# A two-layer graph convolution kernel: row blocks of each h added by an accumulating transfer before the column sums

## The reference, cut to what matters

```python
h = jnp.maximum(_layernorm(x, axis=-1), 0.0)
x = x + _L0_gnn_ref(h, adj, L0_gnn_b1, adj, L0_gnn_b2)

# inside _L0_gnn_ref
fv = x.mean(axis=1)                      # column means of h
nf = fv / norm(fv); sim = nf[:, :, None] * nf[:, None, :]
_, idx = top_k(sim, 9); idx = idx[..., 1:]
adj = zeros.at[b, row, idx].set(1.0); adj = max(adj, adj.T); diag = 1
h = relu(_gc(swapaxes(x), adj, W1, b1))  # (adj / deg) @ (x @ W.T + b)
h = _gc(h, adj, W2, b2)
```

## Time and profile before

| what | value |
|---|---|
| median of 3 runs | 506.15 us (505.9 to 506.9) |
| profiled execution, own time | 505.98 us |
| its span | 503.8 us |
| busy: TensorE, POOL, VectorE, ScalarE | 484.9, 372.7, 357.3, 339.2 us |
| mean granted TensorE clock | 0.992 of full speed |
| moved by DMA | 102.74 MB, 204 GB/s in the mean |

### The profile page before, as it was taken

One profiled execution on the slowest core, in us unless ns is written; L12 is line 12 of the kernel. 1 busy time (PEld: TensorE's weight loads), 2 busy tenths in 40 slices (PEclk: granted clock), 3 DMA queues, 4 the chain that ended last, 5 costly groups with the idle time before them and its releaser, 6 DMA issues.

```text
span 503.8 us, 7367 instructions
## 1 busy us (share of the span) xinstructions
PE 484.9 (96%) x2434; PEld 332.4 (66%) x2434; DVE 357.3 (71%) x891; ACT 339.2 (67%) x699; POOL 372.7 (74%) x343
## 2 busy tenths in 40 slices
PE   1998999999999999999999999999999999999996
PEld 0256577667776777757776777767776677777774
DVE  5999897988776886788776887778766764522334
ACT  4747888658777587757788487758877565545551
POOL 0356549959779697769878697777879697797772
PEclk9997999999999999999999999999999999999999
DMA  8992376356566465646666266646444243444424
GB/s 328 349 378 85 146 272 240 111 220 245 209 251 251 155 241 212 242 164 262 250 246 249 91 260 252 236 183 251 175 169 147 94 160 127 154 167 168 167 85 167
DMA packets 27717, 102.74 MB, mean 204 GB/s; under 512 B 2080, under 2 KB 2592, under 8 KB 27680
## 3 DMA queue, kind: packets, MB, share of 16 engines
q1 hardware_dynamic: 27296, 101.23, 53.0%
q0 software_dynamic: 384, 1.05, 0.6%
HBM read 68.72 MB, written 33.55 MB: 203 GB/s over the span
## 4 chain that ended last, share of the span: by engine, by line
PE 88%; DVE 8%; DMA 2%; ACT 1%; issue 1%; SPq 0%; DVEq 0%; ACTq 0%
PE ps L599 48%; PE ps L605 24%; PE ps L629 5%; PE aux L564 5%; PE aux L660 4%; DVE stats L733 2%; DMA xin<-x 2%; PE aux L588 1%; DVE onehot L818 1%; DVE code_r L798 1%; DVE res L911 1%; PE aux L575 1%; DVE onehot L807 1%; PE ps L636 0%; DVE code L764 0%
## 5 line engine op out<-in xcount | busy, mean ns | idle before, releaser
L474 POOL TENSOR_TENSOR r_lo<-r,r_hi 128x512 fp32r<-128x512 f32 x128 | 162.7, 1294 | 46.8 <-ACT r_hi L383 45.3
L463 POOL TENSOR_TENSOR h_lo<-hb,h_hi 128x512 fp32r<-128x512 f32 x128 | 167.9, 1325 | 7.0 <-ACT h_hi L346 7.0
L911 DVE SCALAR_TENSOR_TENSOR res<-ps,bias,res 128x512 f32<-128x512 f32 x128 | 90.2, 747 | 77.4 <-PE ps L636 77.3
L599 PE MATMUL ps<-r_hi,w_hi 128*128 128x512 f32 x256 | 108.7, 425 | 1.3 <-ACT r_hi L375 1.3
L599 PE MATMUL ps<-h_hi,w_hi 128*128 128x512 f32 x256 | 102.0, 399 | 0.3 <-DVE res L911 0.3
L599 PE MATMUL ps<-r_hi,w_lo 128*128 128x512 f32 x256 | 102.1, 399 | 0.0
L599 PE MATMUL ps<-h_hi,w_lo 128*128 128x512 f32 x256 | 101.3, 396 | 0.0
L324 ACT ACTIVATE hb<-xin,nmean,rstd 128x1024 f32<-128x1024 f32 x64 | 79.0, 1235 | 32.4 <-DVE nmean L754 32.4
L366 ACT ACTIVATE r<-ps,beta 128x512 f32<-128x512 f32 x64 | 43.4, 684 | 74.4 <-PE ps L629 74.4
L733 DVE BATCH_NORM_STATS2 stats<-xin 128x6 f32<-128x512 f32 x128 | 79.1, 678 | 3.8 <-DMA xin<-x 3.8
L605 PE MATMUL ps<-h_lo,w_hi 128*128 128x512 f32 x256 | 73.3, 408 | 0.0
(11 more groups left out here) (94 smaller groups left out, 545.7 us busy)
## 6 DMA issues: line engine op xcount, KB each, us to landing
res<-x SPq DMA_DIRECT2D x32, 1024.0 KB, 4.8
out<-res SPq DMA_DIRECT2D x31, 1024.0 KB, 4.0
xin<-x SPq DMA_DIRECT2D x30, 1024.0 KB, 7.1
xin<-x SPq DMA_DIRECT2D x4, 512.0 KB, 5.1
out<-res SPq DMA_DIRECT2D x4, 256.0 KB, 2.1
w<-w_t SPq DMA_DIRECT2D x1, 256.0 KB, 9.1
cst<-small SPq DMA_DIRECT2D x1, 229.0 KB, 6.9
xg<-x_t,rows POOLq DMA_INDIRECT x8, 4.8
```

What stands on the lines that cost most here:

```text
L463: last = nc.gpsimd.tensor_tensor(h_lo[:, kf, n], hb[:, b % NH, kf, n], h_hi[:, kf, n].bitcast(F32), ALU.subtract)
L474: last = nc.gpsimd.tensor_tensor(r_lo[:, kf, n], r[:, kf, n], r_hi[:, kf, n].bitcast(F32), ALU.subtract)
L599: nc.tensor.matmul(bank[m][:], wt[:, kf, m * P:m * P + P], mov[:, kf, n], start=(kf == 0 and wt is w_hi), stop=False, skip_group_check=True)
L911: nc.vector.scalar_tensor_tensor(res[:, b % NR, m, n], bank[m][:], bias2[:, m:m + 1], res[:, b % NR, m, n], ALU.add, ALU.add).then_inc(out ...
```

## The change

- `column_sums(k)` for k = 2 to 7 streams one block per batch, `h_sum[:, q]`, in place of two. For k = 1 it stays as it was.
- `h_sum` holds four blocks. For each batch from 8 to 31 SP copies the first row block of h into it (`copy_h`, SBUF to SBUF, 512 KB), and POOL issues a transfer that adds the second block to it (`fold`, 512 KB, `accum_op=add`). TensorE waits for the four folds of the group. Before batch 8, h_sum is the load buffer of x of batches 3 and 7.
- The ring of x has three buffers, without those two batches. load_x(11) waits for batch 8 to be normalised, where it waited for batch 7.
- On TensorE `column_sums(k)`, k > 1, stands behind layer2(t, 1).
- ScalarE normalises batch t+9 in step t, behind split_h(t+2, 0) and take_sums, where it normalised batch t+8 at the head of the step. It raises `h_first` after the first block. VectorE's moments and scales run a batch further ahead.
- ScalarE writes `code` and `ZERO` straight from the sums in PSUM (`zeros`: Relu of 0.5 - 2^112 s is 0.5 for a sum of zero and 0 else) and the class codes are renumbered to fit; VectorE's pass for `code` goes. It keeps a small `stat`, now with a row sum, and adds 6 to it in `top_rows`.
- TensorE's waits for take_sums become waits for `zeros`.

The diff without its blank lines and most of its context:

```diff
@@ -19,7 +19,7 @@
 G = 4
-NX = 4
+NX = 3
@@ -47,6 +47,12 @@
+CODES = [1.0, 1.5, 2.0, 3.0, 0.0, 0.5, 6.0, 7.0]
+HALF = 0.5
+STEEP = -(2.0 ** 112)
@@ -59,7 +65,7 @@
     parts = [
-        ("cls", np.where(row < 16, row % 8, -1.0)[:, None]),
+        ("cls", np.where(row < 16, np.array(CODES)[row % 8], -1.0)[:, None]),
@@ -102,6 +108,7 @@
         hb = sb("hb", [P, NH, KF, N])
+        h_sum = sb("h_sum", [P, G, N])
@@ -123,10 +130,12 @@
         eps = sb("eps", [P, 1])
+        half = sb("half", [P, 1])
...
         best = sb("best", [P, 8])
+        stat = sb("stat", [P, K_TOP])
@@ -160,7 +169,7 @@
         STAT = aux[:, at + 72:at + 72 + K_TOP]
-        ZERO = aux[:, at + 80:at + 81]
+        ZERO = aux[:, N - 1:N]
@@ -176,6 +185,17 @@
+        def turn(b):
+            return b - (b > G - 1) - (b > 2 * G - 1)
+        def x_of(b):
+            if b in (G - 1, 2 * G - 1):
+                i = 2 * (b // G)
+                return h_sum[:, i:i + 2]
+            return xin[:, turn(b) % NX]
@@ -196,6 +216,10 @@
         h_ready = sem("h_ready")
+        h_first = sem("h_first")
+        side_loaded = [sem(f"side_loaded{i}") for i in range(2)]
+        copied = [sem(f"copied{q}") for q in range(G)]
+        folded = sem("folded")
@@ -268,9 +292,18 @@
             def load_x(b):
-                if b >= NX:
-                    sp.wait_ge(h_ready, b - NX + 1)
-                sp.dma_start(xin[:, b % NX], x_v[b]).then_inc(x_loaded[b % NX], 16)
+                if b in (G - 1, 2 * G - 1):
+                    sp.dma_start(x_of(b), x_v[b]).then_inc(side_loaded[b // G], 16)
+                else:
+                    if b >= NX:
+                        sp.wait_ge(h_ready, b - NX + (b >= LEAD + NX))
+                    sp.dma_start(x_of(b), x_v[b]).then_inc(x_loaded[turn(b) % NX], 16)
+            def copy_h(b):
+                sp.wait_ge(h_first, b - LEAD + 1)
+                sp.wait_ge(fv_done, 2 * (b // G))
+                sp.dma_start(h_sum[:, b % G], hb[:, b % NH, 0]).then_inc(copied[b % G], 16)
@@ -283,19 +316,26 @@
             sp.dma_start(w[:], w_t.rearrange("(k p) n -> p k n", p=P)).then_inc(w_loaded, 16)
-            load_x(3)
+            load_x(G - 1)
...
             sp.dma_start(bias2[:], b2).then_inc(bias_loaded, 16)
-            for b in range(NX, LEAD):
+            for b in range(G, LEAD):
...
                 load_res(b)
-            for b in range(LEAD, LEAD + NX - 1):
+            for b in range(LEAD, LEAD + NX):
...
             for t in range(NB):
-                if t + LEAD + NX - 1 < NB:
-                    load_x(t + LEAD + NX - 1)
+                if t + LEAD + NX < NB:
+                    load_x(t + LEAD + NX)
+                if t == 1:
+                    copy_h(LEAD)
+                    copy_h(LEAD + 1)
+                if t == 2:
+                    copy_h(LEAD + 2)
+                if 1 < t < NB - LEAD - 1:
+                    copy_h(t + LEAD + 1)
@@ -322,12 +362,14 @@
                 last = nc.scalar.activation(
-                    hb[:, a, kf], xin[:, b % NX, kf], ACT.Relu, bias=nmean[:, kf, e:e + 1],
+                    hb[:, a, kf], x_of(b)[:, kf], ACT.Relu, bias=nmean[:, kf, e:e + 1],
...
                     last.then_inc(h_part, 1)
+                elif b >= LEAD:
+                    last.then_inc(h_first, 1)
@@ -337,6 +379,14 @@
+            def zeros(k):
+                com = dict(bias=half[:], scale=STEEP)
+                act.wait_ge(fv_copied, 3 * k + 3)
+                nc.scalar.activation(code[:, K_TOP + 1:H + 1], aux[:, K_TOP:H], ACT.Relu, **com)
+                nc.scalar.activation(code[:, H + 1:N], aux[:, H:N - 1], ACT.Relu, **com)
+                nc.scalar.activation(ZERO, aux[:, N - 1:N], ACT.Relu, **com).then_inc(zero_ready, 1)
@@ -396,6 +446,7 @@
             split_h(1, 0)
+            zeros(0)
@@ -408,24 +459,30 @@
             for t in range(LAST):
-                if 0 < t < NB - LEAD:
-                    normalise(t + LEAD, 0)
-                    normalise(t + LEAD, 1)
+                if t == 1:
+                    normalise(LEAD + 1, 0)
+                    normalise(LEAD + 1, 1)
...
                     root(7)
+                if t + 2 < NB:
+                    split_h(t + 2, 0)
...
                     take_sums(group_at(t, 0))
-                if t + 2 < NB:
-                    split_h(t + 2, 0)
+                    zeros(group_at(t, 0))
...
                     root(LEAD + 2)
+                elif 1 < t < NB - LEAD - 1:
+                    normalise(t + LEAD + 1, 0)
+                    normalise(t + LEAD + 1, 1)
+                    if t == 2:
+                        root(LEAD + 4)
@@ -434,12 +491,16 @@
                 if t == 0:
+                    zeros(1)
...
                     normalise(LEAD, 1)
+                    root(LEAD + 1)
...
                     root(LEAD + 3)
-                elif t != 2 and t + LEAD + 1 < NB:
-                    root(t + LEAD + 1)
+                    normalise(LEAD + 2, 0)
+                    normalise(LEAD + 2, 1)
+                elif 2 < t < NB - LEAD - 2:
+                    root(t + LEAD + 2)
@@ -482,6 +543,11 @@
+            def fold(b):
+                pool.wait_ge(copied[b % G], 16 * (b // G - 1))
+                pool.wait_ge(h_ready, b + 1)
+                nc.gpsimd.dma_start(h_sum[:, b % G], hb[:, b % NH, 1], accum_op=ALU.add).then_inc(folded, 16)
@@ -532,9 +598,16 @@
                         split_h(3, 0)
+                if t == 1:
+                    fold(LEAD)
+                    fold(LEAD + 1)
+                elif 1 < t < NB - LEAD - 1:
+                    fold(t + LEAD + (t > 2))
...
                     split_h(t + 2, 1)
+                if t == 2:
+                    fold(LEAD + 3)
@@ -555,21 +628,26 @@
             def column_sums(k):
-                pe.wait_ge(h_ready, G * k + G)
+                if k == 1:
+                    pe.wait_ge(h_ready, 2 * G)
+                else:
+                    pe.wait_ge(folded, 16 * G * (k - 1))
                 pe.wait_ge(beta_ready, k)
+                blocks = KF if k == 1 else 1
...
                     n = half_of(h)
-                    for kf in range(KF):
+                    for kf in range(blocks):
                         for q in range(G):
+                            h_all = hb[:, (G + q) % NH, kf, n] if k == 1 else h_sum[:, q, n]
                             last = nc.tensor.matmul(
-                                aux[32 * q:32 * q + 32, n], c_("ones")[:, 0:32], hb[:, (G * k + q) % NH, kf, n],
-                                start=(kf == 0), stop=(kf == KF - 1), tile_position=(0, 32 * q))
+                                aux[32 * q:32 * q + 32, n], c_("ones")[:, 0:32], h_all,
+                                start=(kf == 0), stop=(kf == blocks - 1), tile_position=(0, 32 * q))
...
                 pe.wait_ge(code_ready, 3 * k + 3)
-                pe.wait_ge(fv_copied, 3 * k + 3)
+                pe.wait_ge(zero_ready, k + 1)
@@ -678,7 +756,7 @@
             layer1(0, 1)
-            pe.wait_ge(fv_copied, 3)
+            pe.wait_ge(zero_ready, 1)
@@ -705,9 +783,9 @@
                 add_terms(t, 0)
+                layer2(t, 1)
...
                     column_sums(group_at(t, 0))
-                layer2(t, 1)
@@ -724,13 +802,14 @@
             def spreads(b, kf):
-                a = b % NX
...
                     dve.wait_ge(x_first[b], 16)
+                elif b in (G - 1, 2 * G - 1):
+                    dve.wait_ge(side_loaded[b // G], 16)
                 else:
-                    dve.wait_ge(x_loaded[a], 16 * (b // NX + 1))
+                    dve.wait_ge(x_loaded[turn(b) % NX], 16 * (turn(b) // NX + 1))
                 for h in range(2):
-                    last = nc.vector.bn_stats(stats[:, b % 2, kf, h], xin[:, a, kf, half_of(h)])
+                    last = nc.vector.bn_stats(stats[:, b % 2, kf, h], x_of(b)[:, kf, half_of(h)])
@@ -759,14 +838,14 @@
                 nc.vector.max(best[:], fv[:, 0:N]).then_inc(dve_top, 1)
-                nc.vector.tensor_scalar(STAT, fv[:, 1:K_TOP + 1], 0.0, 6.0, ALU.is_equal, ALU.add)
-                nc.vector.tensor_scalar(ZERO, fv[:, 0:1], 0.0, 4.0, ALU.is_equal, ALU.add).then_inc(static_ready, 1)
-                nc.vector.tensor_scalar(code[:], fv[:, 0:N], 0.0, 4.0, ALU.is_equal, ALU.add).then_inc(zero_ready, 1)
...
                 nc.vector.tensor_copy(first[:, 0:1], best[:, 0:1]).then_inc(dve_top, 1)
+                nc.vector.tensor_scalar(stat[:], fv[:, 1:K_TOP + 1], 0.0, None, ALU.is_equal, ALU.add,
+                                        accum_out=beside[:, 0:1]).then_inc(static_ready, 1)
                 dve.wait_ge(dve_top, 5 * k + 2)
+                dve.wait_ge(static_ready, 2 * k + 1)
@@ -776,6 +855,8 @@
                 nc.vector.max_index(found[:], best[:], fv[:, 0:N]).then_inc(dve_pick, 1)
+                dve.wait_ge(zero_ready, k + 1)
+                nc.vector.tensor_scalar(STAT, stat[:], 6.0, None, ALU.add).then_inc(static_ready, 1)
```

(18 more changed lines are left out.)

## The result

The changed kernel takes 516.4 us (median of 4 runs, 515.7 to 523.3) against 506.0 for the kernel before on the same chip: ratio 1.022, 95% interval 1.018 to 1.027. It is slower, and outside the range. The profiled execution took 516.48 us (514.5 of span), 10.5 more than that of before. Times of later kernels are medians without the odd execution that came out over 1.5% above the fastest of its kernel; each ratio is to the kernel before on the same chip.

What follows compares the result with a forecast made beforehand. TensorE, busy 484.9 of 503.8 us, was taken to bound the kernel. Terms -10.7 - 0.2 + 1.0 + 3.3 + 1.5 + 2.5 = -2.6 took 505.98 to 503.4 us; range 496.5 to 512.

Steps and rivals of the forecast that it cites:

- The start: Group 0: VectorE loses the `code` pass, TensorE's filling products wait for zeros(0); -0.2 us, bounds -0.9 and +0.6.
- rival (b): Sums wait for the folds' landing in every group, at 9 us landing +11.2 us, 517 us; chance 0.2.
- (c): POOL becomes the feeder at 2.0 us a fold; TensorE waits for r_lo, +8 us, 514 us; chance 0.13.
- The gather that the prediction wanted away from `code_r`: POOL's gather no longer meets code_r and takes 1.0 us, so r_lo(13,0) fits by 0.1 us.
- term 1: Column sums: six of seven calls take half, gaining 10.7 us; moving them costs TensorE nothing by itself.
- Terms 1 and 4: Halved column sums, -10.7 us; landing of folds, +3.3 us in group 2 and +2.5 us for near misses.
- Term 3 at t = 1: Issuing two folds in a row on POOL ahead of r_lo(2,1): +1.0 us, 0.3 to 3.
- Landing at 83 to 84: Copies of h 8 and 9, queued on SP behind load_x(11) and others, land at 83 to 84 us.
- `spreads(12)` delays finish(2,1) by some 0.6 us: On VectorE at t=1, spreads(12) ahead of codes(1) delays finish(2,1) by 0.6 us, inside the shift of +1.0 us.
- Loads in a ring of three still land some 8 us ahead: Loads of x in a ring of three buffers still land some 8 us ahead of the moments.
- The two-input pass: VectorE's two-input code_r and POOL exclude each other for a whole instruction; code_r takes 1.2 us, the gather there 1.0 more.
- Term 5, clock: A stall of 3.3 us at 103 us may halve TensorE's clock: +1.5 us, 0 to 2.8.

Runs made afterwards that it cites:

- one-block kernel: The kernel before, with only column_sums(2) to (7) streaming just the first block of each h, no copy or fold: 500.1 us, ratio 0.986.
- store0_first: The changed kernel with SP's load of x(11) put behind the store of batch 0 in place of ahead of it: 512.0 us, ratio 1.011.
- group2_both: The changed kernel without copies and folds for batches 8 to 11, column_sums(2) streaming both blocks: 509.3 us, ratio 1.005.
- last version: The changed kernel without group 2's transfers, x(11) loaded behind store 0, class_terms and top_mark reordered, sums(2) ahead of layer2(3,1): 498.9 us, ratio 0.985.
- the first of the two misses: The changed kernel with the moments of batch 12 moved out of step 2 on VectorE to behind group_sources(1): 522.7 us, ratio 1.032.

## Why the prediction was wrong

**What held.** The sizes of the new operations. A fold takes POOL 0.88 us of issue in the median (forecast 1.0), lands in 5.4 us (5.5), and a one-block call takes 1.90 (1.79). The 5.5 has some luck in it: the prediction put it on shared engines alone, and 1.5 of the 5.4 are the addition, which it didn't price (3.9 without). The start changed by nothing (-0.2). TensorE waits 0.8 us for the folds of group 2 (0.5 more than it waited before, where the forecast had 3.3) and not at all in later groups, so rival (b) did not occur where the change puts the sums. TensorE has no wait for POOL between 120 and 480 us, so (c) did not either; that the time came out near theirs (517 and 514) says nothing for them. The gather that the prediction wanted away from `code_r` does fall from 2.0 to 1.0 us in the one-block kernel, where it starts 0.5 us ahead of `code_r`; in the changed kernel it still takes 1.86 in the median.

**"Moving the call behind layer2(t,1) costs TensorE nothing by itself"** (term 1) was the first step to fail. I looked at TensorE's columns and at who feeds the sums, and not at who reads them: VectorE runs its passes over the sums, four of about 1.2 us, in one piece with class_terms and the table behind them, and the move brings TensorE's next demand for those closer by a layer-2 call. Alone it costs 2.6 us a group; together with the other edits of the changed kernel, 1.2, of which the order on VectorE gives 0.7 back. For the same reason the halved call itself brings 1.1 of its 1.7. Terms 1 and 4 gave -1.29 a group, the runs -0.46.

**Term 3 at t = 1, "+1.0 us (0.3 if the copies are early, 3 if issue is dear)",** is the step that decides the sign: 13.4 us up to layer2(3,1). Three readings in it failed, each by one queue.
- "Landing at 83 to 84" for the copies: 87.8. I knew that store 0 would stand behind the later load, and named it, but priced only the copies, each as if alone. The four transfers of 3 MB that leave from 77.5 to 79 fill the DMA engines (share 0.95 of the stretch from 80 to 90 us, 0.71 before). x 12 takes 8.3 us, but 8.4 without the copies too: what makes it late is that it is issued 10.4 us later.
- "`spreads(12)` delays finish(2,1) by some 0.6 us": its own duration, without its wait for x 12, and without table(2), which the edit puts behind it. "Loads in a ring of three still land some 8 us ahead" holds for steady steps; this one landed 5.3 us late. Store 0 ahead of that load removes it (store0_first).
- The two-input pass. The prediction names the rule of the Trainium skill (SBUF — State Buffer, "Who interferes with whom") and used it for what `code_r` does to POOL. The runs show the other direction and a larger size: with POOL working without a gap, the `code_r` of group 1 took 8.3 to 8.6 us in five kernels with early folds. It took 2.2 to 2.3 in the kernel before and the two made from it, and 1.2 to 1.6 in the six others. In eleven of these fourteen traces, the five long ones among them, it ends 1.1 us behind the last subtraction ahead of POOL's first pause or issue. The trace agrees with the rule that the two exclude each other; that the wait can last over several of POOL's instructions is this case's. It doesn't always: in two kernels without folds there (the changed kernel without any transfers, and the one without those of group 2) `code_r` took 1.4 us in the middle of a pair of subtractions, which then lasted 3.5 us. What decides between the two is open.

**Term 5, clock.** Half clock from 85.5 to 92.3 and from 102.6 to 109.4 us. It comes with the waits, as forecast, only that there were two such stretches, some 4.2 us in all where the forecast had 1.5.

The loss of the opening, by experiments: some 7 us of the whole time are there only with group 2's transfers (group2_both), some 4 are the late x 12 (store0_first, and the wait of 4.43 that stays in group2_both). At the start of the sums of group 2 the two are 9.1 and 5.5 us, more than the 13.9 lost there, so they overlap. That both together with 0.7 us a group from VectorE's order account for the way from 516.4 to 498.9 is shown by the last version, not by adding the single effects: taken alone, two of the repairs made it slower.

## What to carry to other kernels

When a call moves, walk the engines that read its result as well as those that feed it: the long call may be the cover of a chain on another engine, and halving it or moving it lays that chain bare. Price an opening separately from the steady loop: there one late load holds a store, the store the next load, and new transfers meet it all at once; leaving the new method out of the first group where it applies was worth more here than any reordering. Where a stall came from full DMA engines, moving its waiter didn't help in either of two trials; taking transfers away did.

## What the runs showed of the hardware beyond that

- A VectorE pass with two inputs, 1.21 us when POOL is idle (the first of the two misses), lasted 8.62 us beside POOL's gapless subtractions of two inputs, and ended 1.1 us behind the first pause. POOL lost nothing by it: without the addition its pairs took 2.53 us beside a pass of 8.28.
- Behind an accumulating transfer that POOL has issued, its pairs of subtractions took 2.83 us instead of 2.54, VectorE's pass beside them or not. Over the execution they average 1.40 us a subtraction, against 1.29 with plain transfers in the same places; what slows them isn't shown.
- The accumulating transfer of 512 KB between two places of SBUF costs 0.88 us of issue against 0.58 plain, and lands in 5.4 us against 3.9. In total POOL's queue, folds and gathers, takes 14.7% of the span's 16 engines for 13.6 MB, where the other queue moves 113.8 MB in 57.5%: twice the engine time per byte. With plain transfers in place of the folds it takes 6.7% for the same bytes.
- While both folds of step 1 were under way, the DMA engines were full and moved little: 268 GB/s from 90 to 92 us at a share of 1.08, against 420 just before at 1.02.
